# A token-routed kernel on one core: shorter table of loads, four id writes moved into the last round of stage 1, and gathers spread over the scatters

## The reference

```
h  = layernorm(x)
q, k, v = split(rms_norm(h) @ w_qkv.T)           # three of 512x512
q, k = rms_norm(q), rms_norm(k)
y  = cumsum(exp(k) * v) / (cumsum(exp(k)) + 1e-6) * sigmoid(q)
u, g = split(y @ w_swiglu.T)                     # two of 512x512
x1 = x + h + (u * silu(g)) @ w_out.T             # one of 512x512
t  = layernorm(x1)
best two of 8 experts per token, by softmax(t @ router_weight.T + router_bias)
out = x1 + t + sum over the two experts e of (t @ weight[e] + bias[e])
```

## Time and profile before

| what | value |
| --- | --- |
| median of three runs | 1638.11 us |
| the profiled execution's own time | 1636.89 us |
| its span | 1635.1 us |
| mean granted clock of TensorE | 0.993 |
| busy: PE, PEld, DVE | 96%, 79%, 74% |
| busy: ACT, POOL | 35%, 61% |
| DMA traffic | 258.57 MB, 158 GB/s on average |
| pair weight loads on SP | 93 issues of 2048 KB, many of them conditional |

### The profile page before, as it was taken

The page is one execution under the profiler, slowest core; times in us unless marked ns, Lnnn a source line. Parts: engine busy times, 40 slices in busy tenths (PEclk is TensorE's granted clock), DMA queues, the critical chain, the costliest instruction groups (busy, mean ns, idle before and its releaser), DMA issues.

```text
span 1635.1 us, 27374 instructions
## 1 busy us (share of the span) xinstructions
PE 1572.5 (96%) x7987; PEld 1284.8 (79%) x7987; DVE 1214.4 (74%) x2436; ACT 570.6 (35%) x1088; POOL 993.6 (61%) x1253
## 2 busy tenths in 40 slices
PE   8899999999999999999999999989999867899998
PEld 5788888888888888888888888778788755677786
DVE  7777778877877788778777877897887564565665
ACT  4333333333333333333333333323333222333433
POOL 2546666675577667765766586567663365565663
PEclk9999999999999999999999999999999989999999
DMA  6122333334333343333433343343425587599884
GB/s 234 49 93 91 128 134 126 122 127 147 117 117 117 117 142 127 135 123 132 152 117 117 117 143 116 117 143 117 143 98 188 175 269 227 161 368 372 317 312 178
DMA packets 135387, 258.57 MB, mean 158 GB/s; under 512 B 18519, under 2 KB 19297, under 8 KB 135242
## 3 DMA queue, kind: packets, MB, share of 16 engines
q1 hardware_dynamic: 118442, 222.62, 39.3%
q0 software_dynamic: 16800, 34.21, 6.3%
HBM read 321.00 MB, written 101.11 MB: 258 GB/s over the span
## 4 chain that ended last, share of the span: by engine, by line
PE 87%; DVE 3%; another core or an unknown queue 2%; SPq 2%; issue 2%; DMA 1%; ACT 1%; POOL 0%; POOLq 0%; DVEq 0%; ACTq 0%
PE pU L1348 4%; PE pG L1348 3%; PE pV L1348 3%; PE pG L1350 3%; PE pK L1348 3%; PE pO L1350 3%; PE pO L1348 3%; PE pO L1349 3%; PE pK L1350 3%; PE pG L1349 3%; PE pK L1349 3%; PE pV L1349 3%; PE pV L1350 3%; PE pQ L1348 3%; PE pQ L1349 3%; PE pQ L1350 3%
## 5 line engine op out<-in xcount | busy, mean ns | idle before, releaser
L784 DVE RECIPROCAL B<-B 128x512 f32<-128x512 f32 x64 | 214.6, 3353 | 2.2
L388 POOL TENSOR_SCALAR sa<-ss,hinv,ep 128x1 f32<-128x1 f32 x128 | 44.0, 344 | 238.7 <-ACT B L576 238.2
L402 POOL TENSOR_TENSOR F<-B,F 128x512 fp32r<-128x512 f32 x64 | 82.6, 1290 | 140.5 <-ACT F L598 140.5
L473 POOL DMA_INDIRECT out_dram<-B,tab x91 | 93.8, 1031 | 110.7 <-DVE B L866 66.0
L812 DVE SCALAR_TENSOR_TENSOR B<-B,nm,pO 128x512 f32<-128x512 f32 x64 | 47.8, 746 | 146.5 <-PE pO L1350 146.5
L433 POOL TENSOR_TENSOR R<-B,R 128x512 fp32r<-128x512 f32 x112 | 142.6, 1297 | 0.0
L428 POOL TENSOR_TENSOR B<-B 128x512 f32<-128x512 f32 x112 | 141.8, 1292 | 0.0
L1348 PE MATMUL pK<-R,F 128*128 128x512 f32 x256 | 106.3, 415 | 2.0 <-DVE F L744 2.0
L1348 PE MATMUL pG<-R,F 128*128 128x512 f32 x256 | 106.4, 416 | 1.5 <-POOL F L402 1.4
L1348 PE MATMUL pU<-R,F 128*128 128x512 f32 x256 | 106.3, 415 | 0.0
L1348 PE MATMUL pV<-R,F 128*128 128x512 f32 x256 | 101.4, 396 | 1.5 <-DVE B L758 1.5
(11 more groups left out here) (256 smaller groups left out, 4535.5 us busy)
## 6 DMA issues: line engine op xcount, KB each, us to landing
R<-pair_weights SPq DMA_DIRECT2D x93, 2048.0 KB, 11.7
pair_weights<-R SPq DMA_DIRECT2D x112, 512.0 KB, 3.9
B<-in_wm SPq DMA_DIRECT2D x112, 256.0 KB
B<-pair_biases SPq DMA_DIRECT2D x93, 256.0 KB, 12.4
x_scratch<-B SPq DMA_DIRECT2D x64, 264.0 KB
B<-in_x SPq DMA_DIRECT2D x64, 256.0 KB
B<-in_xt SPq DMA_DIRECT2D x32, 256.0 KB
XTB<-in_xt SPq DMA_DIRECT2D x32, 256.0 KB
```

What stands on the lines that cost most here:

```text
L388: p.tensor_scalar(sa[:, r, j:j + 1], ss[:, r, j:j + 1], hinv[:, 0:1], ep[:, r:r + 1], ALU.mult, ALU.add).then_inc(s[f"ra{j}"], 1)
L402: p.tensor_tensor(fr(3)[0], DD, fr(2)[1], ALU.subtract).then_inc(s["yl"], 1)
L473: p.indirect_dma_start(od, bass.IndirectOffsetOnAxis(ap=idx[:, J:J + 1], axis=0), YO[J % 4], None, bounds_check=T * 128 - 1, oob_is_err=Fa ...
L784: v.reciprocal(DD, DD).then_inc(s["rec"], 1)
```

## The change

Three things are changed.

1. The table of loads. Its first row (`tc`) holds the number of the pair, with 64 (SKIP) added where nothing new is to be loaded; such an index lies outside `pair_weights`, and the DMA is issued with a bounds check that skips it entirely, in place of a condition. The second row (`tw`) holds the slot times 4096, which PE can use as it is; a shift by three gives the place of the bias. The bounds assertions of the table reads are gone, SP reads two words rather than one and unpacks nothing. So that slot and bias place fit, the blocks of the buffer are renamed. DVE's side work for the table has as many steps as before, with one small operation more in `slots_of`.
2. At the end of round i = 63, behind gather 7, places 52 to 55 are sent. They no longer stand at J = 3.
3. For J under 16 one gather follows a scatter, not two: gather 10 at J = 3, and so on to gather 19 at J = 12, where it stands behind the second `read_ids`. From J = 16 on there are two as before.

```
             def load_pair(t):
...
-                code = e.value_load(tc[0:1, t:t + 1], min_val=0, max_val=NP * 16 - 1)
-                slot, new, pair = code & 7, (code >> 3) & 1, code >> 4
-                e.dma_start(Rf[:, bass.ds(slot * 4096, 4096)],
+                pair, at = e.value_load(tc[0:1, t:t + 1]), e.value_load(tw[0:1, t:t + 1])
+                e.dma_start(Rf[:, bass.ds(at, 4096)],
                             pwd[bass.ds(pair, 1), :, :].rearrange("o p n -> p (o n)"),
-                            cond=new, max_dma_last_dim=2048).then_inc(dwb[(t - 2) % 8], 16)
+                            bounds_check="skip_entire_dma", max_dma_last_dim=2048).then_inc(dwb[(t - 2) % 8], 16)
...
-                e.dma_start(B[:, bass.ds(((slot + 2) & 7) * 512, 512)], pbd[bass.ds(pair, 1), :].broadcast_to([128, H]),
-                            cond=new).then_inc(dwb[(t - 2) % 8], 16)
+                e.dma_start(B[:, bass.ds(at >> 3, 512)], pbd[bass.ds(pair, 1), :].broadcast_to([128, H]),
+                            bounds_check="skip_entire_dma").then_inc(dwb[(t - 2) % 8], 16)
...
                 if i >= Z - 3:
                     gather(2 * (i - Z + 3))
                     gather(2 * (i - Z + 3) + 1)
+                if i == Z:
+                    while sent < BLK * (NB - 1):
+                        place(sent)
+                        sent += 1
             yl(Z)
             x2n(Z - 1)
             gather(8)
...
-                for _ in range(2):
+                for _ in range(2 if J >= NEAR else 1):
                     if asked < min(J + NXG, EARLY if J < NEAR else NJ):
                         gather(asked)
                         asked += 1
...
-                return ((v.value_load(tw[0:1, J:J + 1], min_val=0, max_val=7) + 2) & 7) * 512
+                return v.value_load(tw[0:1, J:J + 1]) >> 3
...
-                v.scalar_tensor_tensor(out=q4[:, 2, :], in0=c, scalar=-8.0, in1=runq[:, :],
+                v.scalar_tensor_tensor(out=c, in0=c, scalar=-8.0, in1=runq[:, :],
                                        op0=ALU.mult, op1=ALU.add).then_inc(s["rt"], 1)
...
-                v.scalar_tensor_tensor(out=q4[:, 1, :], in0=qnum[:, :], scalar=16.0, in1=q4[:, 2, :],
-                                       op0=ALU.mult, op1=ALU.add).then_inc(s["rt"], 1)
+                v.tensor_scalar(q4[:, 2, :], c, 4096.0, None, ALU.mult)
+                v.tensor_scalar(q4[:, 1, :], qnum[:, :], SKIP, None, ALU.add).then_inc(s["rt"], 1)
...
-                at = pe.value_load(tw[0:1, J:J + 1], min_val=0, max_val=7) * 4096
+                at = pe.value_load(tw[0:1, J:J + 1])
```

More of the change, by code:

```diff
@@ L23 @@
 NSR = 8
+SKIP = 64.0
 def build_program(nc, x, xt, wq, wk, wv, wu, wg, wo, wm, bm, wr, br, consts, out):
@@ L70, in build_program @@
         Rf, Ff = R[:, :].bitcast(f32), F[:, :].bitcast(f32)
-        X = [blk(0), blk(1), blk(2)]
-        WT, KVT, EQT, DD = blk(4), blk(5), blk(6), blk(7)
-        XT = [blk(3), sb("XTB", [128, 512])[:, :]]
+        X = [blk(6), blk(7), blk(0)]
+        WT, KVT, EQT, DD = blk(2), blk(3), blk(4), blk(5)
+        XT = [blk(1), sb("XTB", [128, 512])[:, :]]
         CW, CKV, TH_, S1 = blk(8), blk(9), blk(10), blk(11)
@@ L286, in load_run @@
                 slot = (6 + r) % 8
-                code = e.value_load(rc[0:1, r:r + 1], min_val=0, max_val=2 * NP - 1)
+                pair = e.value_load(rc[0:1, r:r + 1])
                 e.dma_start(Rf[:, slot * 4096:(slot + 1) * 4096],
[L289 to L292, removed]
+                            pwd[bass.ds(pair, 1), :, :].rearrange("o p n -> p (o n)"),
+                            bounds_check="skip_entire_dma", max_dma_last_dim=2048).then_inc(drun[r // 2], 16)
+                e.dma_start(blk(slot), pbd[bass.ds(pair, 1), :].broadcast_to([128, H]),
+                            bounds_check="skip_entire_dma").then_inc(drun[r // 2], 16)
             def load_pair(t):
@@ L1074, in table @@
                     ready()
-                    v.scalar_tensor_tensor(out=ge, in0=qnum[:, :], scalar=0.5, in1=ge,
+                    v.scalar_tensor_tensor(out=ge, in0=qnum[:, :], scalar=-SKIP, in1=ge,
                                            op0=ALU.add, op1=ALU.mult).then_inc(s["rt"], 1)
@@ L1081, in table @@
                     ready()
-                    v.scalar_tensor_tensor(out=ge, in0=ge, scalar=2.0, in1=c,
-                                           op0=ALU.mult, op1=ALU.mult).then_inc(s["rt"], 1)
+                    v.tensor_tensor(ge, ge, c, ALU.mult).then_inc(s["rt"], 1)
                     yield
@@ L1113, in table @@
                 ready()
-                v.scalar_tensor_tensor(out=col, in0=c4[:, 3:4], scalar=8.0, in1=c4[:, 1:2],
+                v.scalar_tensor_tensor(out=col, in0=c4[:, 3:4], scalar=-SKIP, in1=c4[:, 1:2],
                                        op0=ALU.mult, op1=ALU.add).then_inc(s["rt"], 1)
@@ L1125, in table @@
                     ready()
-                    v.tensor_copy(rc[:, :], pX[0:1, 480:484]).then_inc(s["rt"], 1)
+                    v.tensor_scalar(rc[:, :], pX[0:1, 480:484], SKIP, None, ALU.add).then_inc(s["rt"], 1)
                 yield "table"
```

## The result

The changed kernel takes 1724.71 us (median of five runs, 1724.1 to 1726.83) where the kernel before takes 1638.11 (1635.35 to 1638.89 in five runs beside it): a ratio of 1.0529, 95% interval 1.0517 to 1.0542. It is 86.6 us slower. The profiled execution has a span of 1722.2 us. The prediction was 1631.6, with 1639.3 as the upper end of its range, so it was wrong in direction and far outside.

A forecast was written before the change was run, and what follows sets the result against it. TensorE was 96% busy, with losses at the stage 1 to 2 passage, where POOL's DMA trains delay PE's signals. Terms -7.7 + 1.3 + 0.9 - 1.0 = -6.5 us gave 1631.6; range 1626.4 to 1639.3.

The forecast's parts named there:

- The short table: Table reads and load issues: fewer SP steps per load, -1.0 us, bounds 0 and -3; PE and DVE reads counted at nothing.
- Rival (4): SP in late tiles: skipping a load by bounds costs more than by condition; +41 us, 1673; chance 0.06.
- The gathers: Stage 1 to 2 passage: one gather per scatter shortens a POOL train, -7.7 us; a later, longer train costs +1.3.
- train B: POOL's thirteen unbroken indirect DMAs from 1304.17 to 1321.6; to shrink to five, so PE's signals come earlier, -7.7 us.
- train A: POOL's six unbroken indirect DMAs, 1265.21 to 1272.8: four places, gathers 6 and 7; four more places to be appended.
- The signs of being right: Five-DMA train from 1304, ya(5) near 1315, mm(7) 1319, mm(11) 1338, L611 1274.6; from 1485 on, all shifted 6 us.
- Places 52 to 55: Last round of stage 1: four DMAs appended to train A delay PE's signal, +0.9 us, bounds 0 and +5.1.
- rival (1): Train A holds PE's signal to its end: total -2.3 us, 1635.8; sign L611 at 1278 or later; chance 0.20.
- train C: POOL's thirteen unbroken DMAs, 1337.82 to 1354.4; a signal came 4.2 us late in its middle; one DMA more, +1.3 us.
- The rule against the change: DMA engines take one ring's descriptors in order; fewer gathers ahead only land a scatter sooner, so the 7.7 us would not come.

The follow-up runs named there:

- the run with half of the checks: Kernel before with a second PE table read, without bounds, for the low weights' addresses only; high weights keep the bounded read: 1664.62 us, ratio 1.0132.
- the three orders beside it: Kernel with places in the gap, with: places 56-63 two a round; no DVE bounds; two a round plus fewer late gathers. Ratios 0.9995, 0.9996, 0.9997.
- the kernel without DVE's bounds: Kernel with places in the gap, but no bounds in DVE's table read: 1619.84 us, ratio 0.9996.
- places in the gap: Changed kernel with bounds named in PE's and DVE's table reads, places 52 to 55 sent behind scatter 1: 1633.96 us, ratio 0.9937.

## Why the prediction was wrong, point by point

**The step that failed** is in "The short table": "The reads of the same table by PE (L1481) and DVE (L848) lose a step each too; they run ahead of the work they serve and are counted at nothing." The diff's `value_load(tw[...])` without bounds was read as less work, because the assertion behind the read goes. It does go. But the bounds were also what made the addresses cheap, and the check comes back at each address, inside the twelve matmuls, and from mm(20) on a tile's time is PE's. The term taken at 0 measures +86.5 us when it stands alone (1731.05 against 1644.56). The view that could have warned was there and not read: L1495's own register instructions, 46 ns each, and the 0.69 us that three matmuls leave for them. That room, and the form of a check behind the read at L1481 (151 and 18 ns), were there to be worked out: two more checks of 0.39 us do not fit, one does, as the run with half of the checks shows.

**Rival (4), the slower one,** had the right sign and the wrong engine; that its +41 us lie nearest to the result is luck. It put a cost of the new form of the load on SP; SP's skipped issues stayed at about 0.09 us.

**The gathers.** Forecast -7.7 at mm(11), with the short train B. With train A kept as it was, the runs show -8.3 (1337.15 for 1345.41), and tile 7 taken over without a hold. The signs of being right came there too: a train of five from 1304.8, mm(7) at 1318.39 and mm(11) at 1337.15, for "near 1319" and "near 1338". It takes the shorter train B of both moves: the gathers spread alone, with the places left in it, gained nothing (0.9994). So the term was right for executions in which signals are held. Where nothing is held it is worth nothing: the kernel before at 1620 shows no loss to the three orders beside it.

**Places 52 to 55.** Forecast +0.9, bounds 0 and +5.1. With PE's bounds given back mm(1) starts at 1283.91 and POOL's L402 at 1286.64, against 1281.68: +5.0. That is the time of rival (1), though not its sign (L611 at 1278 or later): of the two late take-overs the first (L615, 1276.98) still came inside the train and 3.3 us later than before, the second (L637, 1279.85) 1.6 us behind its end. In the profile of the changed kernel itself the first was not held at all and the second came inside the train, which ends at 1278.9, and L402 was 3.4 us later than before:

```profile
1271.88 0.60 ACT L615 ACTIVATE F<-pH 128x512 fp32r<-128x512 f32 x1 [0.70 <-PE pH L1335]
...
1276.82 0.60 ACT L637 ACTIVATE R<-pU 128x512 fp32r<-128x512 f32 x1 [3.64 <-remote]
```

So the term measures +3.4 to +5.0 where +0.9 was taken. The row it was taken from, the hold in the middle of train C, is one that does not come each time. The gap of 8.7 us behind scatter 1 takes the same four DMAs for nothing.

**The sum without the failed step.** Forecast -6.5 us, or -2.3 by rival (1); measured 0.9986, -2.3 us with an interval of -4.6 to 0. The agreement with rival (1) to the tenth is luck, given that interval. In the changed kernel itself nothing of the passage's gain is left at mm(11), whose first matmuls start up to 1.4 us apart with PE waiting for its own queue, at a granted clock of 0.54 from 1345 to 1360 (0.80 before):

```profile
1345.99 0.79 PE L1498 MATMUL pQ<-R,F 128*128 x1 [1.52 <-DVE B L870]
1347.26 0.76 PE L1499 MATMUL pQ<-R,F 128*128 x1 [0.47 <-issue]
1348.69 0.77 PE L1501 MATMUL pQ<-R,F 128*128 x1 [0.67 <-issue]
```

The register instructions there last up to 0.7 us each (the maxima of L1498 and L1501 above), and PE has more of them than before.

**The rule against the change** (Trainium skill, DMA: Bandwidth & Descriptors, Queues, rings and completion order) is not touched by the result: no run shows when a scatter lands against the gathers ahead of it. Its landing is waited for by SP's L367 at the end in every profile, and otherwise only by DVE in the kernel without DVE's bounds, twice, 5.5 us in all.

## What to carry to other kernels

A dynamic address inside a row of matmuls must come from a register whose bounds are stated, or be worked out once ahead of them (the second was not tried here); a diff that drops `min_val` and `max_val` adds instructions, it does not remove them. When an engine is the limit, count its sequencer's instructions for each matmul against the matmul's own time, in the view that includes register instructions, since PE's busy share cannot show it: below the budget they are free, above it they set the pace. A gain read from one profile's waits is worth an execution elsewhere before it is believed: here it was 0.6% in one group of runs and nothing in another.

## What the runs showed of the hardware that was not expected

The kernel before took 1638, 1645 and 1643 us in some groups of runs and 1620 in another, with less than 1% between most runs of a group. The profiles near 1640 us and those near 1620 differ in one thing that shows at once. In the former register instructions are stretched to 0.7 us (54 of SP's last between 0.6 and 0.8 us in the kernel before), and signals of PE are taken over late. Of those 54 and one of PE, 54 begin within 0.4 us of one of POOL's indirect DMAs; but with that margin these fill 80% of stage 2, so this alone says little. In the three profiles near 1620 there is not one such instruction. One instruction of SP, L311's move, with places in the gap (1634 us) and then without DVE's bounds (1620 us):

```profile
L311 SPq MOVE B<-pair_biases x89: 3/29/1099, 1274.9 to 1602.5; - x89
```

```profile
L311 SPq MOVE B<-pair_biases x89: 29/29/37, 1274.4 to 1586.7; - x89
```

A move between registers waits for nothing in the program, so what stretches it is outside the kernel's own waits. Late signals and stretched instructions come and go together, which makes one cause for both likely; what it is, no run here shows. Against one particular chip as the cause speaks that the runs carry the same chip number (6) in the group at 1620.2 us and, four minutes later, in the last one at 1642.7, whose profile has the late signals and 52 such instructions of SP again.

The two kernels just compared have the same order on POOL: the one at 1620 is 0.5 us ahead at mm(11) (1336.65 for 1337.15), 8.7 at mm(42) (1451.56 for 1460.25) and 16.1 at mm(90) (1607.27 for 1623.34). So most of the difference comes behind the passage. Their windows from 1425 to 1485 show DMA at work for the whole time in both, with 383 GB/s in the one at 1620 and 370 in the other. All three profiles near 1620 have 383 to 386 GB/s there, those of the other groups, where PE has its bounds, 343 to 375: transfers are faster too.
